# Row tiles for the two heads of a pair in the score matmuls of a gated cross-attention block

## The reference

```python
x = x + tanh(g_xattn) * attention(layernorm(x), ctx, ctx)   # 16 heads of 16 features
x = x + tanh(g_ffn)   * ffn(layernorm(x))                   # 256 -> 1024 -> 256, relu

# attention
q = xpos((layernorm(x) @ Wq.T + bq) * 0.25);  k = xpos(ctx @ Wk.T + bk);  v = ctx @ Wv.T + bv
out = softmax(q @ k.T) @ v  per head, then @ Wo.T + bo
# each ffn layer: base linear + 3 softmax-gated LoRA experts of rank 8
```

## Time and profile before

| | us |
|---|---|
| median of 3 runs | 623.74 |
| lowest and highest | 620.21, 624.2 |
| profiled execution: its span, first to last instruction | 622.0 |

### The profile page before, as it was taken

How to read it: one execution, slowest core, us unless ns; L and a number is a source line. 1 busy time by engine, 2 the same in 40 slices (tenths; PEclk the granted TensorE clock), 3 DMA queues, 4 the chain that set the end, 5 groups by cost and what they waited for, 6 DMA issues and landing times.

```text
span 622.0 us, 9354 instructions
## 1 busy us (share of the span) xinstructions
PE 536.2 (86%) x3424; PEld 407.4 (66%) x3424; DVE 431.1 (69%) x960; ACT 256.8 (41%) x405; POOL 86.0 (14%) x121
## 2 busy tenths in 40 slices
PE   2668845999989998989989998999899998989795
PEld 1546434856976497735976497747886597649574
DVE  4576376958987498846987497958987578645423
ACT  3242524454435434352445525364436443452220
POOL 2426012011201021011101021011201110001000
PEclk9865977999999999989999998999999999999698
DMA  7301000010001010200101010011001000200000
GB/s 273 109 2 36 1 34 1 1 46 4 33 2 70 1 35 2 71 9 6 35 2 70 1 35 2 36 45 35 1 1 71 0 2 1 71 1 1 2 34 35
DMA packets 6140, 18.86 MB, mean 30 GB/s; under 512 B 932, under 2 KB 1772, under 8 KB 5964
## 3 DMA queue, kind: packets, MB, share of 16 engines
q10 hardware_dynamic: 4005, 12.53, 5.7%
q1 hardware_dynamic: 2087, 5.68, 2.7%
HBM read 13.76 MB, written 4.19 MB: 29 GB/s over the span
## 4 chain that ended last, share of the span: by engine, by line
PE 60%; DVE 22%; ACT 9%; issue 6%; ACTq 1%; POOL 1%; DMA 1%; DVEq 0%
PE psF L1058 11%; PE psF L1118 10%; PE psX L1105 6%; ACT probs L528 4%; PE psX L1164 4%; DVE max_t L741 4%; PE psX L977 3%; PE psX L994 3%; PE psO L1178 3%; PE psO L1181 3%; PE psF L1178 2%; PE psF L1181 2%; PE psF L1064 2%; DVE heads_t L774 2%; PE psX L1091 2%
## 5 line engine op out<-in xcount | busy, mean ns | idle before, releaser
L741 DVE TENSOR_REDUCE max_t<-psX 128x4 fp32r<-128x616 f32 x128 | 99.6, 795 | 6.1 <-PE psX L1105 3.0
L528 ACT ACTIVATE probs<-psX 128x1024 f32<-128x1024 f32 x64 | 64.0, 1024 | 52.4 <-PE psX L1164 52.4
L1118 PE MATMUL psF<-w_hi,h_hi 128*128 128x284 f32 x256 | 76.9, 300 | 2.4 <-DVE h_lo L734 1.5
L1118 PE MATMUL psF<-w_lo,h_hi 128*128 128x284 f32 x256 | 75.1, 293 | 0.0
L1118 PE MATMUL psF<-w_hi,h_lo 128*128 128x284 f32 x256 | 74.9, 293 | 0.0
L1105 PE MATMUL psX<-km,qT 96*128 96x308 f32 x256 | 65.2, 341 | 7.4 <-DVE max_t L741 4.5
L1105 PEld LDWEIGHTS psX<-km,qT 96*128 96x128 f32 x256 | 48.7, 204 | 24.1 <-DVE max_t L741 12.8
L438 ACT ACTIVATE h_hi<-psF 128x512 fp32r<-128x512 f32 x64 | 37.3, 595 | 63.1 <-PE psF L1064 62.7
L734 DVE SCALAR_TENSOR_TENSOR h_lo<-psF,h_hi 128x512 fp32r<-128x512 f32 x64 | 43.7, 684 | 16.7 <-ACT h_hi L438 16.7
L1118 PEld LDWEIGHTS psF<-w_hi,h_hi 128*128 128x128 f32 x256 | 48.2, 188 | 7.9 <-issue 4.6
L1058 PE MATMUL psF<-xT_lo,w_hi 128*128 128x512 f32 x128 | 51.1, 410 | 0.0
(11 more groups left out here) (155 smaller groups left out, 1047.5 us busy)
## 6 DMA issues: line engine op xcount, KB each, us to landing
x<-in_x_dram ACTq DMA_DIRECT2D x8, 512.0 KB, 3.3
x_ln<-in_x_dram ACTq DMA_DIRECT2D x7, 512.0 KB, 3.3
out_dram<-x ACTq DMA_DIRECT2D x7, 512.0 KB, 2.7
heads_t<-in_w_dram SPq DMA_DIRECT2D x1, 1024.0 KB, 8.2
heads_t<-in_w_dram SPq DMA_DIRECT2D x1, 994.0 KB, 4.7
tab<-in_tables_dram SPq DMA_DIRECT2D x1, 674.0 KB, 6.6
x_ln<-in_x_dram SPq DMA_DIRECT2D x1, 512.0 KB, 3.4
wkv_sb<-in_wkv_dram SPq DMA_DIRECT2D x1, 512.0 KB, 9.4
```

Source lines behind the costliest of these rows:

```text
L528: nc.scalar.activation(dst, psX[:, 2 * (i % 2):2 * (i % 2) + 2, :], ACT.Exp).then_inc(sc_exp.sem, 1)
L741: V.tensor_reduce(max_t[:, k, half, :].rearrange("p (h g) -> p g h", h=2)[:, 2 * j:2 * j + 2, :], psX[:, 2 * j:2 * j + 2, 0:2 * S].rearran ...
L1118: ins = mm(psF[:, F_OF_K[k], 0:W2N], a[:, m, tokens(k)], w[:, m, :], start=m == 0 and i == 0, stop=m == HT - 1 and i == 2)
```

## The change

Each head gets 64 rows of its own (`HR`): 48 rows for its three parts (`KS`), one for the maximum or the one (`KA` = 49), and 15 of padding. A pair has 128 rows, head 0 from row 0 and head 1 from row 64. No mask is needed; keys are written once. In the first pass a call has four matmuls of 154 columns over 48 rows instead of two of 308 over 96; the two heads of a pair read different row halves and write different banks. In the second pass a main step still has two matmuls of 512 columns, now over 49 rows at row 0 or row 64. The "rest" steps use rows 0 to 112.

```diff
-KS = 96
-KA = KS + 2
+HR = 64
+KS = 3 * D
+KA = KS + 1
+KP = HR + KA
...
-        split = sb("split", [P, TT * NG * KS], F32R)
+        split = sb("split", [P, TT * H * HR], F32R)
+        qh = split[:, :].rearrange("p (a r) -> p a r", r=HR)
...
-        qT = sb("qT", [KA, NG, CH], F32R)
+        qT = sb("qT", [P, NG, CH], F32R)
...
-        km = sb("km", [KA, NG, 2, S], F32R)
+        km = sb("km", [P, NG, S], F32R)
...
-        ctxT = sb("ctxT", [P, FT, S])
+        ctxT = xn[:, 2:4, :].rearrange("p k e -> p (k e)")[:, 0:FT * S].rearrange("p (f s) -> p f s", f=FT)
...
-                        sp.dma_start(qT[KS + hh:KS + hh + 1, 4 * f:4 * f + 4, :].bitcast(F32),
+                        sp.dma_start(qT[HR * hh + KS:HR * hh + KA, 4 * f:4 * f + 4, :].bitcast(F32),
...
+            nc.gpsimd.memset(qh[:, :, KS:HR].bitcast(F32), 0.0).then_inc(pad_ready.sem, 1)
...
-                for lo, done in ((0, q_hi), (64, q_hi2)):
-                    copy(split[:, :].rearrange("p (a r) -> p a r", r=KS)[:, :, lo:lo + 32],
-                         q_rc.rearrange("p k (g r) -> p (k g) r", r=32)).then_inc(done.sem, 1)
+                for lo, done in ((0, q_hi), (2 * D, q_hi2)):
+                    copy(qh[:, :, lo:lo + D], q_rc.rearrange("p k (h d) -> p (k h) d", d=D)).then_inc(done.sem, 1)
...
-                for hh in range(2):
-                    V.tensor_scalar(km[:, 0:4, hh, 0:P], psX[0:KA, 2, :].rearrange("p (g s) -> p g s", g=4),
-                                    mask[0:KA, hh:hh + 1], None, ALU.mult).then_inc(km_v.sem, 1)
+                V.tensor_copy(km[:, 0:4, 0:P], psX[:, 2, :].rearrange("p (g s) -> p g s", g=4)).then_inc(km_v.sem, 1)
...
                 V.tensor_reduce(max_t[:, k, half, :]
...
-                                psX[:, 2 * j:2 * j + 2, 0:2 * S].rearrange("p g (h s) -> p g h s", h=2),
+                                psX[:, 2 * j:2 * j + 2, 0:2 * S].rearrange("p h (g s) -> p h g s", g=2),
...
-                for g in range(4 * half + 2 * j, 4 * half + 2 * j + 2):
-                    ins = mm(psX[:, g % 4, 0:2 * S], qT[0:KS, g, tokens(k)],
-                             km[0:KS, g, :, :].rearrange("p h s -> p (h s)"), start=True, stop=True)
+                for n in range(2):
+                    g = 4 * half + 2 * j + n
+                    for hh in range(2):
+                        rows = slice(HR * hh, HR * hh + KS)
+                        ins = mm(psX[:, 2 * j + hh, S * n:S * n + S], qT[rows, g, tokens(k)], km[rows, g, :],
+                                 start=True, stop=True)
...
-                        ins = mm(o_ps, km[:, n // 2, j, 0:P], qT[:, n // 2, :], start=True, stop=True)
+                        rows = slice(HR * j, HR * j + KA)
+                        ins = mm(o_ps, km[rows, n // 2, 0:P], qT[rows, n // 2, :], start=True, stop=True)
```

More of the change, by code:

```diff
@@ L174, in build @@
         const_v = count("const_v", 1)
+        pad_ready = count("pad_ready", 1)
         gate_ready = count("gate_ready", 1)
@@ L423, in key_operands @@
                 act.wait_ge(km_ps.sem, km_ps.at(b, 2))
+                copy(km[:, 4:8, 0:P], psX[:, 3, :].rearrange("p (g s) -> p g s", g=4)).then_inc(km_a.sem, 1)
+                act.wait_ge(km_ps.sem, km_ps.at(b, 3))
+                rest = psO[:, 0:NG * 32].rearrange("p (g s) -> p g s", g=NG)[:, :, 0:SR]
                 for hh in range(2):
[L425 to L428, removed]
-                for hh in range(2):
+                    rows = slice(HR * hh, HR * hh + HR)
                     for a in range(2):
-                        ins = copy(kr[:, a::2, 64 * a + 32 * hh:64 * a + 32 * hh + SR], rest[:, a::2, :],
-                                   scale=mask[0:KA, hh:hh + 1])
+                        ins = copy(kr[rows, a::2, 64 * a + 32 * hh:64 * a + 32 * hh + SR], rest[rows, a::2, :])
                     ins.then_inc(km_a.sem, 1)
@@ L491, in step @@
                     act.wait_ge(qT_ps.sem, qT_ps.at(c, g + 1))
-                    copy(qT[0:KS, g, :], psX[0:KS, g % 4, :]).then_inc(qT_a.sem, 1)
+                    copy(qT[:, g, :], psX[:, g % 4, :]).then_inc(qT_a.sem, 1)
                     if full and g == 0:
@@ L706, in rotate_keys @@
                 dve.wait_ge(k_rot.sem, k_rot.at(b, 4))
[L707 to L710, removed]
+                kf = k_rc.rearrange("p a (h d) -> p (a h) d", d=D)
+                V.tensor_copy(kh[:, :, 0:2 * D].rearrange("p a (t d) -> p a t d", t=2),
+                              kf.unsqueeze(2).to_broadcast([P, 2 * H, 2, D])).then_inc(k_split.sem, 1)
                 dve.wait_ge(k_split.sem, k_split.at(b, 1))
[L712 removed]
+                V.tensor_tensor(kh[:, :, 2 * D:KS], kf, kh[:, :, 0:D].bitcast(F32), ALU.subtract).then_inc(k_split.sem, 1)
             def key_operands(b):
                 dve.wait_ge(km_ps.sem, km_ps.at(b, 1))
[L717 to L719 removed]
+                V.tensor_copy(km[:, 0:4, 0:P], psX[:, 2, :].rearrange("p (g s) -> p g s", g=4)).then_inc(km_v.sem, 1)
                 dve.wait_ge(km_a.sem, km_a.at(b))
[L722 to L724 removed]
+                V.tensor_copy(km[:, :, P:S], psO[:, 0:NG * 32].rearrange("p (g s) -> p g s", g=NG)[:, :, 0:SR]
+                              ).then_inc(km_v.sem, 1)
             def q_transposed(c, g):
                 dve.wait_ge(qT_ps.sem, qT_ps.at(c, g + 1))
[L729 removed]
+                V.tensor_copy(qT[:, g, :], psX[:, g % 4, :]).then_inc(qT_v.sem, 1)
             def h_low(d, m):
@@ L740, in reduce_max @@
                 dve.wait_ge(max_ps.sem, max_ps.at(c, i + 1))
-                V.tensor_reduce(max_t[:, k, half, :].rearrange("p (h g) -> p g h", h=2)[:, 2 * j:2 * j + 2, :],
-                                psX[:, 2 * j:2 * j + 2, 0:2 * S].rearrange("p g (h s) -> p g h s", h=2),
+                V.tensor_reduce(max_t[:, k, half, :].rearrange("p (h g) -> p h g", h=2)[:, :, 2 * j:2 * j + 2],
+                                psX[:, 2 * j:2 * j + 2, 0:2 * S].rearrange("p h (g s) -> p h g s", g=2),
                                 AX.X, ALU.max).then_inc(max_red.sem, 1)
@@ L881, in _ @@
             ln1_stats(0)
-            V.memset(ks[:, :, :, KS:KA].bitcast(F32), 1.0).then_inc(const_v.sem, 1)
+            V.memset(kh[:, :, KS:KA].bitcast(F32), 1.0)
+            V.memset(kh[:, :, KA:HR].bitcast(F32), 0.0).then_inc(const_v.sem, 1)
             V.memset(kr[:, :, :].bitcast(F32), 0.0).then_inc(const_v.sem, 1)
@@ L1069, in key_transposes @@
                 for g in range(NG):
-                    ins = nc.tensor.transpose(psX[0:KA, 2 + g // 4, tokens(g % 4)].bitcast(F32R), ks[:, 0, g, :], ident_r[:, :])
+                    ins = nc.tensor.transpose(psX[:, 2 + g // 4, tokens(g % 4)].bitcast(F32R), ks[:, 0, g, :], ident_r[:, :])
                     if g % 4 == 3:
@@ L1080, in q_transposes @@
                 if g == 0:
+                    if first:
+                        pe.wait_ge(pad_ready.sem, 1)
                     pe.wait_ge(q_lo.sem, q_lo.at(c))
@@ L1090, in q_transposes @@
                 for k in range(TT):
-                    ins = nc.tensor.transpose(psX[0:KS, g % 4, tokens(k)].bitcast(F32R), qs[:, k, g, :], ident_r[:, :])
+                    ins = nc.tensor.transpose(psX[:, g % 4, tokens(k)].bitcast(F32R), qs[:, k, g, :], ident_r[:, :])
                 ins.then_inc(qT_ps.sem, 1)
@@ L1337, in position_tables @@
     ck, sk = (t.reshape(P, -1) for t in cs(pos, True))
-    r = np.arange(P)
-    head = np.where(r < KS, (r % 32) // D, r - KS)
-    mask = np.stack([(head == 0), (head == 1)], 1).astype(f)
-    return np.concatenate([cq, sq, ck, sk], 1).astype(f), mask
+    return np.concatenate([cq, sq, ck, sk], 1).astype(f)
 def kernel(**inputs):
@@ L1372 @@
         lora[r + NL] = bias
-    pos, mask = position_tables()
+    pos = position_tables()
     rows = _np.concatenate([i["L0_xattn_bq"][perm], i["L0_xattn_bk"][perm], i["L0_xattn_bv"], i["L0_xattn_bo"],
                             i["g_xattn"], i["g_ffn"]])
-    tables = _np.concatenate([pos, _np.broadcast_to(rows, (P, rows.size)), mask], 1)
+    tables = _np.concatenate([pos, _np.broadcast_to(rows, (P, rows.size))], 1)
     arrays = {"x": i["x"], "ctx": i["ctx_1024"], "wq": wq, "wkv": wkv, "wo": wo, "w1": w1, "w2": w2, "a1": a1,
```

23 lines of the change are left out of this document (11 added, 12 removed).

## The result

| | before | changed |
|---|---|---|
| median of the runs, us | 622.02 (4 runs) | 647.14 (4 runs) |
| span of the profiled execution, us | 622.0 | 645.6 |
| ratio, 95% interval | | 1.040 (1.037 to 1.043) |

A forecast was written before the change was run, and what follows sets the result against it. TensorE was taken as the bound (busy 86%, 60% of the chain). Max pass +26 and -1.5, main scores -6, key operands -2 make +16.5 on 622.0: 638.5, plus 1.7 for the median: 640 us, range 620 to 664.

The forecast's parts named there:

- The switch of tile size: Max pass: each call becomes a 64-row island among 128-row work, with two switches at 0.20 us each.
- the idle time before the reductions: Max stages, VectorE: idle time before max_t was to rise from 6 to some 35 us.
- Overlap of the row tiles: Max calls: matmuls of both row tiles stream together, 0.07 us a round instead of 0.14; their loads are concurrent too.
- 0.18 us for two rounds: Max call: the second round waits for its weights, so both rounds take 0.11 + 0.07 us.
- The sum for the max pass: Calls go from 0.28 to 0.58 us: +3.7 us a stage, +26 in seven stages; -1.5 in the first chunk.
- Rival (b): Max pass: no cost for switching between 64 and 128 rows; 605 us in all, chance 10%.
- rival (c): Max pass: half a switch, the load fetched during the drain, call 0.38 us; 621 us in all, chance 11%.
- rival (d): Max pass: heads of a pair run one after the other with the whole array, +15 us; 636 in all, chance 4%.
- The main scores: Score stages: two 512-column matmuls become one round, -8.6 us on the chain, +2.6 for new switches; net -6 us.
- the last sentence on the clock: Seven max stages: gaps at every switch might lower the granted clock, which would only add time; no size given.
- At nothing: Terms expected to cost nothing, among them wider query transposes, whose matmul covers the load; bound 0 to 2.6 us.
- The key operands: Key copies in four chunks: VectorE and ScalarE lose copies, about -1.0 us in the first, 0.3 in each other; together -2.

The follow-up runs named there:

- tiny48: Kernel before the change plus one two-column matmul over 48 rows (a 64-row tile) at the head of each max call; 663.1 us, one run.
- same_tile: Changed kernel with all four matmuls of a max call reading rows 0 to 47, so in one row tile; 678.5 us, one run.
- pairs: Changed kernel with two max calls back to back, then the hidden matmuls of both: 7 islands a stage instead of 13; 628.7 us, ratio 1.012.
- tr112: Changed kernel with query transposes 112 columns wide instead of 128 and their copies 112 rows high; 646.9 us, one run.
- doubled: Changed kernel with every main score matmul issued twice into the same banks; 647.5 us, ratio 1.040.
- mainwhole: Changed kernel with the main scores back to whole-array matmuls over 113 rows, key blocks with zeros; max pass still in row tiles; 648.9 us, ratio 1.0445.

## Why the prediction was right, and where it was not

**The switch of tile size** was the step that decided, and it held: 0.20 us, read from 26-row transposes in a trace that had no 64-row tile, and 0.20 us by tiny48. The pair of calls was forecast at 2.8 us and took 2.77. Of its signs, the idle time before the reductions was forecast too high: 25.0 us, not 35.

**Overlap of the row tiles**, taken from the column tiles, held (same_tile). The 0.18 us for two rounds did as well: 0.38 from the call to what follows, less 0.20 for a switch, which is no separate measurement; but two more rounds in pairs cost 0.22 (0.60 instead of 0.38), twice the 0.11 of a load.

**The sum for the max pass** was forecast at 26 us in seven stages and -1.5 in the first; it was 23.8 and -1.4. Twelve calls at +0.29 are 3.5, and the measured +3.4 a stage is a little under it. Rival (b), no price for a switch, is refuted by pairs and tiny48; rival (c), half a price, would have needed 2.39 us for the pair; rival (d) by same_tile. The -1.4 is partly luck: the first max stage had a clock of 0.60 after the change, in place of 0.50. In tr112, at 0.50, the same stage takes 14.6 us, so the shorter calls are worth 0.8 us there and the clock the rest.

**The main scores** are the term that was mis-sized: -6 forecast, +1.3 measured over the stages. The mechanism is right: pieces at 0.43 us where I said 0.45, and the three stages with a clock of 1.00 before and after 0.7 to 0.8 us shorter, which would be 6 us for eight. What failed is the last sentence on the clock: I looked at the max stages, where gaps "might" cost it, and all seven stayed at 1.00. It fell in score stages. Five of them lost 0.4 to 2.4 us against that 0.75, 7.3 us together, for three reasons. The third and fifth (2.4 us) lost their clock behind longer waits for the exps, which is the change's own doing: it leaves TensorE less to do beside an unchanged chain of exps. The fourth and sixth (2.8 us) lost it after waits for the context's transfer; the kernel before lost it in its fourth stage too, after a wait behind that transfer's issue, and had no such wait in its sixth. Whether the change makes these waits more frequent is not shown: the changed kernel issues them 0.9 and 1.4 us after the start of these stages, and so does doubled, which has no such wait. The first (2.2 us) went from 0.84 to 0.69, and filling the waits did not bring that back (0.71 in doubled); why is open. That the clock follows TensorE's waits is supported by doubled, by mainwhole and by the count over all traces; that it always does is refuted by six stages.

**At nothing** I had put the transposes, with a bound of 2.6 us. My reason, that 128 streamed columns cover the load of 128, was wrong: 0.066, 0.071 and 0.078 us for 96, 112 and 128 columns. But the 3 us of work that this makes lie beside waits, and the time shows 0.03 to 0.13 us a chunk of them. **The key operands'** -2 us did not come as forecast. Before the third and seventh chunk, at full clock in both kernels, the stretches with key copies are unchanged (34.6 us), where I expected 0.3 less each; the first max stage starts 0.4 us earlier, where I expected 1.0.

Together, by the spans: 638.5 forecast and 645.6 measured. The 7.1 us are 7.3 in the score stages and 1.9 between the stages (-2 forecast, -0.1 measured), less 2.1 in the max pass (24.5 forecast, 22.4 measured). The range held because the term that decided was right; the score term was off by more than the whole of its gain.

## What to carry to other kernels

Before matmuls are packed into tiles, count how often the tile size changes: here a round trip costs 0.4 us, more than the 0.14 us of streaming that a call could save, and halving the number of islands gave back 18 of 25 us. The old trace had the price already, in the 26-row transposes between full matmuls. Where TensorE waits in a ring of engines that wait for each other, cutting its work may cost the clock, as in two stages here. Moving independent matmuls ahead of the wait gave 11 us; shortening those behind it gave nothing in sum. And before a lost clock is put down to a change, look at what TensorE waited for in front of it: twice here it was a transfer that came late, which kernels without the change have too.

## What the runs showed of the hardware that was not expected

A transpose of fp32r data costs more the wider its stationary operand, with the same 128 columns streamed: 0.066, 0.071 and 0.078 us for 96, 112 and 128. And 64 more rounds of matmuls left the time where it was (647.5 against 647.1): they cost 1.1 to 1.2 us in the second and the seventh stage, at full clock in both, and the granted clock stayed at 1.00 in four score stages where it had fallen. In two of these four a wait behind the context's transfer was gone as well.
